# Attention on one Trainium2 core: the maximum pass regrouped into 20 pairs of equal shape

## What is computed

```
h   = layernorm(x) * (1 + ca) + sa
q   = rope(h @ Wq), k = rope(h @ Wk), v = h @ Wv      # 32 query heads, 8 key heads, 32 wide
att = q k^T / sqrt(32), causal mask; probs = softmax(att)
x   = x + ga * ((probs v) @ Wo)
h   = layernorm(x) * (1 + cb) + sb
x   = x + gb * (h @ W^T + bias + LoRA(h))
```

## Time and profile before

| | us |
|---|---|
| median of 3 runs | 2511.86 (2506.41 to 2514.66) |
| span of the profiled execution, first to last instruction | 2510.1 |
| TensorE matmul busy in it | 2433.2 (97%) |
| VectorE busy | 1698.5 (68%) |
| GpSimd busy | 1650.9 (66%) |
| ScalarE busy | 1046.8 (42%) |
| mean granted TensorE clock, share of full speed | 0.990 |

### The profile page before, as it was taken

The page is one execution under the profiler, slowest core; times in us unless marked ns, Lnnn a source line. Parts: engine busy times, 40 slices in busy tenths (PEclk is TensorE's granted clock), DMA queues, the critical chain, the costliest instruction groups (busy, mean ns, idle before and its releaser), DMA issues. The chain is left out here.

```text
span 2510.1 us, 36950 instructions
## 1 busy us (share of the span) xinstructions
PE 2433.2 (97%) x13716; PEld 1678.6 (67%) x13716; DVE 1698.5 (68%) x2878; ACT 1046.8 (42%) x1873; POOL 1650.9 (66%) x865
## 2 busy tenths in 40 slices
PE   5999999999999999999999999998999999999998
PEld 3788888887555555555555555554688788888886
DVE  4766666677888887888878888873655354455553
ACT  3433333331666666666666666665211111111111
POOL 3743333341798998999989999993755455555543
PEclk9999999999999999999999999999999999999999
DMA  6532333351535325344233334312433333333330
GB/s 229 201 118 85 115 113 116 122 155 72 161 99 145 73 66 160 82 114 108 66 89 82 82 94 137 82 48 93 134 97 96 100 94 101 110 93 100 110 93 25
DMA packets 179727, 267.49 MB, mean 107 GB/s; under 512 B 20508, under 2 KB 113884, under 8 KB 178400
## 3 DMA queue, kind: packets, MB, share of 16 engines
q1 hardware_dynamic: 179552, 265.13, 36.0%
HBM read 183.22 MB, written 80.81 MB: 105 GB/s over the span
## 5 line engine op out<-in xcount | busy, mean ns | idle before, releaser
L1072 POOL TENSOR_TENSOR p_sum<-p_sum,p_ring 128x1024 f32<-128x1024 f32 (+2 forms) x465 | 991.4, 2159 | 81.0 <-PE ctx_ps L1133 59.7
L263 DVE TENSOR_REDUCE neg_max<-scores_q 128x1 f32<-128x512 f32 (+1 forms) x1168 | 708.7, 655 | 124.0 <-PE scores_q L250 66.0
L966 ACT ACTIVATE p_ring<-scores 128x512 f32<-128x512 f32 (+1 forms) x896 | 453.0, 565 | 243.1 <-DVE scores L1020 178.6
L250 PE MATMUL scores_q<-k_stack,q_stack 96*128 96x512 f32 (+1 forms) x1473 | 442.6, 380 | 3.0 <-DVE neg_max L263 2.0
L1112 PE MATMUL scores<-q_stack,k_stack 98*128 98x512 f32 (+1 forms) x1216 | 423.6, 425 | 12.3 <-ACT p_ring L966 8.8
L617 POOL TENSOR_TENSOR roped_hilo<-roped_hilo 128x512 fp32r<-128x512 f32 x80 | 105.8, 1322 | 339.7 <-ACT roped_hilo L459 339.7
L1112 PEld LDWEIGHTS scores<-q_stack,k_stack 98*128 98x128 f32 x1216 | 198.4, 192 | 175.4 <-ACT p_ring L966 93.2
L250 PEld LDWEIGHTS scores_q<-k_stack,q_stack 96*128 96x128 f32 x1473 | 266.2, 192 | 71.2 <-DVE neg_max L263 36.3
L666 PE MATMUL proj_ps<-h_hi,w_hi 128*128 128x512 f32 x752 | 300.3, 399 | 0.7 <-POOL w_lo L606 0.7
L666 PE MATMUL proj_ps<-h_hi,w_lo 128*128 128x512 f32 x752 | 294.3, 391 | 0.0
L666 PE MATMUL proj_ps<-h_lo,w_hi 128*128 128x512 f32 x752 | 293.6, 390 | 0.0
(11 more groups left out here) (178 smaller groups left out, 3709.9 us busy)
## 6 DMA issues: line engine op xcount, KB each, us to landing
q_stack<-qk_t SPq DMA_DIRECT2D x96, 512.0 KB, 6.9
qk_t<-roped_hilo SPq DMA_DIRECT2D x80, 512.0 KB, 2.8
x_in<-in_L_attn_resid SPq DMA_DIRECT2D x32, 512.0 KB, 6.3
ctx_t<-ctx_raw SPq DMA_DIRECT2D x64, 256.0 KB, 5.6
prefetched<-in_L_wmod SPq DMA_DIRECT2D x4, 4096.0 KB, 13.3
prefetched<-ctx_t SPq DMA_DIRECT2D x31, 512.0 KB, 4.1
prefetched<-inv_t SPq DMA_DIRECT2D x124, 128.0 KB, 5.5
k_stack<-qk_t SPq DMA_DIRECT2D x96, 128.0 KB, 8.8
```

The costliest lines, as they stand in the source:

```text
L250: last = nc.tensor.matmul(dst[:, a, :], qs[0:MHI, h, i * P:(i + 1) * P], ks[0:MHI, lo:lo + w], start=not first and (a == 0 or not diag), s ...
L263: nc.vector.tensor_reduce(sh.negm[:, lo // HALF, hs[0]:hs[-1] + 1, i:i + 1], src, AX.X, ALU.max, negate=True).then_inc(sh.s_mx.sem, 1)
L966: nc.scalar.activation(p[:, a * per:(a + 1) * per, :], src[:, a * per:(a + 1) * per, :], ACT.Exp, scale=SM_SCALE).then_inc(s_ex.sem, 1)
L1072: nc.gpsimd.tensor_tensor(a, a, probs(n, u), ALU.add).then_inc(s_ap.sem, 1)
```

## The change

Equal neighbours among the 38 units are put together into 20 lists, 18 pairs and two single units (0 and 15, those with w of 128): [0], [1,2], [3,4], [5,6], [7,8], [9,10], [11,12], [13,14], [15], [16,17], ... [36,37]. One list goes to each tick, from tick -5 on. For TensorE `max_scores` now does a whole list: first the score products of both units, each after its wait for a bank, then the mask products of both. The two mask products of 512 columns, which stood before their score products, stand behind them as well. VectorE's steps are as before, in the new ticks. The tick of single units is 3 (unit 15) and 15 (unit 0) in place of 4 and 14. `FIRST_MAXIMA` has 47 units in place of 48; there the mask follows each unit's own products.

```diff
@@ -98,7 +98,15 @@
 QUARTER = D // 4
 
 
-MAX_TICK = [m * NE // NM - AHEAD for m in range(NM)]
+MAX_PAIRS = []
+for _m, _u in enumerate(MAX_UNITS):
+    if MAX_PAIRS and len(MAX_PAIRS[-1]) == 1 and MAX_UNITS[_m - 1][:3] == _u[:3]:
+        MAX_PAIRS[-1].append(_m)
+    else:
+        MAX_PAIRS.append([_m])
+assert len(MAX_PAIRS) == NE
+PAIR_FROM = {p[0]: p for p in MAX_PAIRS}
+MAX_TICK = [t - AHEAD for t, p in enumerate(MAX_PAIRS) for m in p]
 
 
 def group_steps(n):
@@ -239,19 +247,29 @@
                      sh.mrow[G * TT * i:G * TT * (i + 1), :].bitcast(F32)).then_inc(sh.s_mr[n % QS].sem, 16)
 
 
+def max_rows(sh, bank, m):
+
+    i, lo, w, hs, diag = MAX_UNITS[m]
+    return bank[:, 0:len(hs) * w].rearrange("p (h n) -> p h n", h=len(hs))
+
+
 def max_product(nc, sh, qs, ks, bank, m):
 
     i, lo, w, hs, diag = MAX_UNITS[m]
-    dst = bank[:, 0:len(hs) * w].rearrange("p (h n) -> p h n", h=len(hs))
-    first = diag and w == P
-    if first:
-        nc.tensor.matmul(dst[:, :, :], sh.identr, sh.maskS[:, 0:len(hs), :], start=True, stop=False)
+    dst = max_rows(sh, bank, m)
     for a, h in enumerate(hs):
         last = nc.tensor.matmul(dst[:, a, :], qs[0:MHI, h, i * P:(i + 1) * P], ks[0:MHI, lo:lo + w],
-                                start=not first and (a == 0 or not diag), stop=not diag or first and a == len(hs) - 1)
-    if diag and not first:
-        last = nc.tensor.matmul(dst[:, :, w - P:w], sh.identr, sh.maskS[:, 0:len(hs), :], start=False, stop=True)
-    last.then_inc(sh.s_p1.sem, 1)
+                                start=(a == 0 or not diag), stop=not diag)
+    if not diag:
+        last.then_inc(sh.s_p1.sem, 1)
+
+
+def max_mask(nc, sh, bank, m):
+
+    i, lo, w, hs, diag = MAX_UNITS[m]
+    if diag:
+        nc.tensor.matmul(max_rows(sh, bank, m)[:, :, w - P:w], sh.identr, sh.maskS[:, 0:len(hs), :], start=False, stop=True
+                         ).then_inc(sh.s_p1.sem, 1)
 
 
 def max_reduce(nc, dve, sh, bank, n, m):
@@ -680,6 +698,7 @@
                 if i >= len(max_banks):
                     pe.wait_ge(sh.s_mx.sem, sh.s_mx.at(i - len(max_banks) + 1))
                 max_product(nc, sh, sh.qs[n], sh.ks[n], max_banks[i % len(max_banks)], m)
+                max_mask(nc, sh, max_banks[i % len(max_banks)], m)
                 if i == TURN_FIRST:
                     pe.wait_ge(sh.s_ml.sem, sh.s_ml.at(1))
                     pe.wait_ge(s_vc.sem, s_vc.at(2 * HB))
@@ -1113,11 +1132,14 @@
                                             qs[n % QS][0:KS, h0:h0 + per, lo:lo + w], start=True, stop=True)
                 last.then_inc(s_p2.sem, 1)
 
-            def max_scores(n, m):
-                if m == 0:
-                    pe.wait_ge(s_st[n % QS].sem, s_st[n % QS].at(n // QS + 1))
-                wait_bank(pe, ("max", n, m))
-                max_product(nc, sh, qs[n % QS], ks[n % QS], mp[BANK[("max", n, m)]], m)
+            def max_scores(n, pair):
+                for m in pair:
+                    if m == 0:
+                        pe.wait_ge(s_st[n % QS].sem, s_st[n % QS].at(n // QS + 1))
+                    wait_bank(pe, ("max", n, m))
+                    max_product(nc, sh, qs[n % QS], ks[n % QS], mp[BANK[("max", n, m)]], m)
+                for m in pair:
+                    max_mask(nc, sh, mp[BANK[("max", n, m)]], m)
 
             def values(n, q):
                 hf, j, hs, lo, w = EXP_UNITS[QUADS[q][0]]
@@ -1186,8 +1208,8 @@
                     scores(n, step[2])
                 elif kind == "mod":
                     mod(n)
-                elif kind == "max":
-                    max_scores(n, step[2])
+                elif kind == "max" and step[2] in PAIR_FROM:
+                    max_scores(n, PAIR_FROM[step[2]])
                 elif kind == "values":
                     values(n, step[2])
                 elif kind == "sum" and n < NG - 1:
```

## The result

The changed kernel takes 2560.79 us (median of 4 runs, 2558.37 to 2561.07); the kernel before took 2509.14 in the 4 runs beside it. The ratio is 1.0212, with a 95% interval of 1.0191 to 1.0233: slower, by about 2%. The forecast was 2558, in a range of 2520 to 2578.

The account below looks back on a forecast made before the run. TensorE, busy 987 of 1000 us in attention, was taken to set the pace, with thin cover on the banks. 1.55 us a group over 30 periods is 46.5; 2510.1 + 46.5 + 1.8 = 2558 us, range 2520 to 2578.

Parts of the forecast that it names:

- The price of a mask after a mask: On TensorE, start to start of two masks in a row: 0.07 us for 128 columns, 0.12 for 256.
- The saving of 0.4 a group: First masks of 8 pairs of 128 columns cost 0.07 in place of 0.12: 12 us in all if TensorE never waits.
- Ticks 0 and 1, 6 and 7, 17 to 19: Masked pairs release their first bank later, so the value step comes later: +0.21, +0.22 and +0.30 us a group.
- Ticks 2 to 5: Unit 19 waits for unit 16, reduced behind tick 4's 512-column addition; value step at 8.30, not 7.59: +0.50 us new here.
- The sum: All ticks of a group together: 1.58 us, taken as 1.55, over 30 periods 46.5 us.
- The other ticks: Estimates for ticks 8 and 9, 10 and 11, 12 to 15, and 16: +0.35 us a group in round numbers.
- Faster: Rival: TensorE alone decides, the gap between mask and next product saves 0.4 a group, 2500 us; chance 0.08.
- no change: Rival: savings and waits cancel, or later starts are swallowed in waits that are there anyway, 2512 us; chance 0.07.
- Half the loss: Rival: ticks 0 to 5 as worked, the rest absorbed, 21 us more, so 2533 us; chance 0.2.
- M to M costs 0.12 or over: Rival: mask to mask on TensorE costs 0.12 us or over, 15 us more, 2573 us; chance 0.15.
- The signs named beforehand: Trace after: L250 waits over 32.2 us, GpSimd busy about 890 of 1000, turns about 36 apart, tick 5's value step at 8.3.
- Where the waits would be longest: TensorE's L250 loads would wait longer for VectorE than 32.2 us, most in ticks 1, 5, 7 and 19.

Follow-up runs that it names:

- half reduces: VectorE reduces only the first half of each maximum unit's columns: 2477.97 us on the kernel before, 2477.93 us on the changed kernel.
- Late masks alone: Kernel before with its old ticks; where both units of a tick carry a mask, the masks stand behind both units' products: 2512.35 us, ratio 1.0017.
- either half alone: Against the kernel before: new ticks with each mask directly behind its unit's products, 2537.22 us; or old ticks with masks late, 2512.35 us.
- another order: Changed kernel with unit 16 moved from tick 4 to tick 3, so the single unit is in tick 4: 2536.35 us, ratio 1.0121.
- another kernel: Kernel before with unit 17 moved from tick 3 to tick 4, so tick 3 has a single unit: 2527.83 us, ratio 1.0085.

## Why the prediction was right

**The bound.** That TensorE sets the pace, with thin cover on the banks, was right. TensorE did no more work; its weight loads waited 90 us longer for VectorE's maxima in 1000 us of attention, and with half reduces the loss was gone.

**The price of a mask after a mask.** Taken as 0.07 for 128 columns and 0.12 for 256; it is 0.068 and 0.121. The saving of 0.4 a group was too small to matter, as worked.

**Ticks 0 and 1, 6 and 7, 17 to 19.** +0.21, +0.22 and +0.30 forecast; +0.21, +0.25 and +0.25 measured. Late masks alone gave the last term by itself, +0.30. Ticks 0, 1, 6 and 7 need both halves of the change: with either half alone ticks 1 and 7 are as before.

**Ticks 2 to 5.** +0.50 forecast, +0.46 measured. The cause that was named, the bank behind the 512-column addition, was shown by moving one unit in either kernel.

**The sum.** The prediction worked out 1.58 and took 1.55. Turns of the kernel before stand at 1248.72 and 1282.62, 33.90 apart; of the changed kernel at 1280.30 and 1315.73, 35.43. That is 1.53. The other ticks, given as +0.35 from estimates of +0.08, +0.10, +0.08 and +0.11, measure +0.14 in 8 and 9, +0.09 in 10 and 11, +0.05 in 12 to 15 and +0.10 in 16: 0.38 together.

**What the sum lacked.** The three groups with a reciprocal. The forecast used one price for all 30 periods. There the later bank met VectorE's 1.74 us reciprocal, the idle gap grew, and the clock fell; those groups cost 2 us more than the others, 6 in all. Half of it went unnoticed in the total because the rest of the kernel came out some 3 us shorter between its ends than before. The start was also off: the prediction added 46 us to 2511.9, while the kernel before, run beside the changed one, took 2509.1, so the loss to be explained is 52. That 2558 lies only 3 us from 2561 is therefore partly luck.

**The rivals.** "Faster" and "no change" are refuted by the time. "Half the loss" is refuted by the table of stretches, where the late banks cost as worked outside ticks 0 to 5 too. "M to M costs 0.12 or over" is refuted by the 0.07. The signs named beforehand held: the wait of L250, now L261, grew from 32.2 to 122.0, GpSimd was busy 885 (about 890 forecast), turns were 36.2 apart on the average (about 36), and the value step of tick 5 stood 8.26 after tick 0 (8.3). Where the waits would be longest was only in part right: ticks 1, 5, 7 and 19 were named, and in 1000 us the waits add up to 27.0 in tick 5, 19.7 in tick 18, 15.4 in tick 14, 13.8 in tick 19 and 11.5 each in ticks 1 and 7.

## What to carry to other kernels

When one engine fills a few buffers that another empties, ask of every reordering when each buffer is released and what stands ahead of its reader; saving a few hundredths of a microsecond at the writer lost half a microsecond at the reader. A product whose completion is held back until its neighbour is done should not sit where the next stage waits for its buffer. And look at which long instruction of the reader falls between two releases: moving one unit across a single addition was worth 20 and 24 us here, in both directions.

## What was not expected of the hardware

- An idle gap of TensorE of 1.43 us was followed by a value step at half clock, 3.34 us for 1.85; the same gap (1.44 us) in another order was not. The low clock came with the reciprocal's groups in the changed kernel and went when the reciprocal was moved; in another kernel it came behind gaps of 0.48 and 0.69 us in a group without one. What decides is open.
- A bf16 mask product of 128 columns costs 0.07 us when another mask follows it, and 0.12 ahead of an fp32 score product: 0.04 to the product and 0.08 by which that product's step is longer. That the product's weight load is the reason is argued, not shown.
- Making VectorE's reduces half as wide, with TensorE's work untouched, took 30 us from the kernel before. VectorE was 82% busy in attention, TensorE 99%: an engine with a fifth of its time free still held up the one that set the pace.
